# Moving attention heads by DMA into projection layout, and reordering the second layer's front, in a two-layer transformer kernel

## The reference

```
x  = hidden_states                        # 2048 x 256
xn = layernorm(x)
x  = x + attention0(xn) + moe0(xn)        # causal softmax attention, 16 heads of 16; 16 experts, top 2
xn = layernorm(x)
x  = x + attention1(xn) + moe1(xn)        # linear-type attention; 16 experts, top 4, and a shared expert

attention0: q, k, v = xn @ w_qkv.T; softmax(q k / 4, causal) v per head; heads side by side @ w_o.T
moe1:       probs = softmax(xn @ w_router); top 4, their weights divided by their sum
            out = shared / 5 + 4/5 * sum over the 4 chosen experts
```

## Time and profile before

| | us |
|---|---|
| median of 3 runs | 920.88 (918.10 to 924.36) |
| profiled execution, its own time | 918.57 |
| span of the profiled execution | 916.8 |
| stage 1 ends (last copy of ps_o) at | 593.75 |
| stage 2 runs from | 596.51 |
| stage 2 ends, first matmul of stage 3 at | 739.57 |
| granted TensorE clock, mean | 0.962 |

### The profile page before, as it was taken

The page is one execution under the profiler, slowest core; times in us unless marked ns, Lnnn a source line. Parts: engine busy times, 40 slices in busy tenths (PEclk is TensorE's granted clock), DMA queues, the critical chain, the costliest instruction groups (busy, mean ns, idle before and its releaser), DMA issues. The chain is left out here.

```text
span 916.8 us, 16029 instructions
## 1 busy us (share of the span) xinstructions
PE 844.7 (92%) x4769; PEld 455.6 (50%) x4770; DVE 641.0 (70%) x1513; ACT 451.3 (49%) x820; POOL 434.7 (47%) x720
## 2 busy tenths in 40 slices
PE   5888789899999999999999997698899989999997
PEld 3533223334444444444444321187744468878886
DVE  5589799888788888888788893167737524445448
ACT  3643145466666566665666666634113123333347
POOL 3323064613644435445345455401777737778820
PEclk9997598999999999999999999987999989999999
DMA  9744952200271211621111012192252234555566
GB/s 328 213 136 138 217 123 76 86 27 30 90 125 35 65 37 53 118 68 42 59 37 48 30 58 75 41 342 78 95 186 92 81 97 154 155 161 155 156 249 245
DMA packets 61730, 105.41 MB, mean 115 GB/s; under 512 B 12118, under 2 KB 45398, under 8 KB 60886
## 3 DMA queue, kind: packets, MB, share of 16 engines
q1 hardware_dynamic: 41110, 49.57, 19.8%
q0 software_dynamic: 16000, 45.70, 14.8%
q10 hardware_dynamic: 4544, 9.21, 3.3%
HBM read 60.30 MB, written 45.96 MB: 116 GB/s over the span
## 5 line engine op out<-in xcount | busy, mean ns | idle before, releaser
L1143 DVE TENSOR_REDUCE part_max<-ps_row 128x1 f32<-128x512 f32 (+3 forms) x560 | 354.1, 671 | 69.8 <-PE ps_row L1297 40.5
L1013 ACT ACTIVATE probs<-ps_st 128x1024 f32<-128x1024 f32 (+3 forms) x320 | 278.4, 896 | 202.3 <-PE ps_st L1276 201.0
L1201 PE MATMUL ps_o<-probs,v_all 128*17 128x512 f32 (+3 forms) x1280 | 148.5, 536 | 13.9 <-ACT probs L1013 8.5
L1297 PE MATMUL ps_row<-ks,qs 96*128 96x512 bf16 (+3 forms) x320 | 110.5, 380 | 11.7 <-DVE part_max L1143 8.6
L1297 PE MATMUL ps_row<-xt_ks,qs 96*128 96x512 bf16 (+3 forms) x320 | 103.2, 351 | 1.0 <-DVE part_max L1143 0.5
L1540 POOL DMA_INDIRECT yd<-moe_ys,moe_home x79 | 82.3, 1042 | 29.8 <-POOL moe_home L1534 17.2
L1276 PE MATMUL ps_st<-qs,ks 99*128 99x512 bf16 (+3 forms) x320 | 88.9, 360 | 4.4 <-DMA qs<-max_parts 4.2
L1276 PE MATMUL ps_st<-qs,xt_ks 99*128 99x512 bf16 (+3 forms) x320 | 82.8, 348 | 2.1 <-ACT probs L1013 1.3
L1571 PE MATMUL moe_ps_h<-w,moe_xs_t 128*128 x316 | 83.0, 386 | 0.1
L1297 PEld LDWEIGHTS ps_row<-ks,qs 96*128 96x128 bf16 x320 | 32.0, 101 | 93.6 <-DVE part_max L1143 57.2
L885 POOL TENSOR_SCALAR_AFFINE_SELECT probs<-probs 128x256 f32<-128x256 f32 x128 | 52.1, 414 | 49.4 <-ACT probs L1013 48.0
(11 more groups left out here) (290 smaller groups left out, 1349.0 us busy)
## 6 DMA issues: line engine op xcount, KB each, us to landing
moe_xs<-xd SPq DMA_DIRECT2D x79, 129.0 KB
qk_parts<-probs SPq DMA_DIRECT2D x16, 384.0 KB, 3.3
qs<-qk_parts SPq DMA_DIRECT2D x96, 64.0 KB, 2.4
moe_xs<-xd POOLq DMA_DIRECT2D x47, 128.0 KB, 2.4
yd<-moe_ys POOLq DMA_DIRECT2D x47, 128.0 KB, 2.1
xd<-zeros POOLq DMA_DIRECT2D x2, 2048.0 KB, 15.4
moe_w<-in_w ACTq DMA_DIRECT2D x2, 2048.0 KB, 20.1
w<-in_we SPq DMA_DIRECT2D x1, 4096.0 KB, 19.3
```

The source lines that it names most:

```text
L1013: act.activation(probs[:, at % NPB, :, off:CH], ps_st[at % 2][:, :, off:CH], ACT.Exp, scale=HD ** -0.5).then_inc(exp_done, 1)
L1143: dve.tensor_reduce(part_max[reduced % 2][:, h:h + k, i, j:j + 1], bank[:, 0:k * w].rearrange("p (h w) -> p h w", h=k), AX_X, ALU.max).the ...
L1201: mm = pe.matmul(ps_o[32 * q:32 * q + HD + 1, off:CH], m.v_all[:, k, g * HG + q, :], probs[:, (at + q // 2) % NPB, q % 2, off:CH], start=F ...
L1297: mm = pe.matmul(cols, qs[c][0:KROWS, h, i * P:(i + 1) * P], ks[g % 2][0:KROWS, h, j * CH:j * CH + w], start=True, stop=(j < c))
```

## The change

- Stage 1: ACT copies `ps_o` to one small tile `o_now` instead of into `o_t`. SP then moves the four heads by four DMAs to the partitions that the projection wants, and the four rows of divisors by four DMAs to DRAM (`heads_home`); the next copy waits for them. When the two groups of a projection half are there for a chunk (8 "shares" in all), SP gathers the 4096 divisors as 128x32 (`gather`), DVE inverts them in place (`invert`), SP writes them back (`return`) and spreads them over the heads' partitions in eight DMAs (`spread`), and DVE multiplies (`share`). These five steps stand 3, 6, 7, 10 and 13 exps after the pair's end in the list. The last share is done in stage 2. `w_o` is loaded in stage 1, by two DMAs ahead of the first gather.
- Planner: SP is charged 3.6 for the moves, and once all max rows and moe0 tiles are placed, the rank of an exp is 1 in place of 3 or 0.
- Stage 2: the two transposes, the reciprocals, the division and ACT's copy go; PE projects straight from `o_t` in two alternating banks. Router picks come from the logits, the exponential of the 16 x 4 chosen ones is taken once at the end, the counts are summed over the four choices by matmul. Order of PE, DVE and ACT is written anew. SP's large weight loads come after the last share's DMAs. Two shared units move behind the tail.
- The barriers at the ends of stages 1 and 2 no longer drain GpSimd.

```diff
+SHARE_STEPS = (("gather", 3), ("invert", 6), ("return", 7), ("spread", 10), ("share", 13))
+def heads_home(eng, m, g, c):
+    k, half, cs = g // 2, g % 2, slice(c * CH, (c + 1) * CH)
+    for h in range(HG):
+        home = (half * HG + h) * HD
+        eng.dma_start(m.o_t[home:home + HD, 2 * k, cs], m.o_now[32 * h:32 * h + HD, :]).then_inc(m.o_moved, 16)
+    for h in range(HG):
+        eng.dma_start(m.den[k * C + c, (half * HG + h) * CH:(half * HG + h + 1) * CH].unsqueeze(0),
+                      m.o_now[32 * h + HD:32 * h + HD + 1, :]).then_inc(m.o_moved, 16)
+def gather_divisors(eng, m, n):
+    eng.wait_ge(m.o_moved, MOVES * ((2 * k + 1) * C + c + 1))
+    eng.dma_start(m.divisor, m.den[n, :].rearrange("(p j) -> p j", p=P)).then_inc(m.o_hops, 16)
+def return_divisors(eng, m, n):
+    eng.wait_ge(m.inverted, n + 1)
+    eng.dma_start(m.rec[n, :].rearrange("(p j) -> p j", p=P), m.divisor).then_inc(m.o_hops, 16)
+def spread_divisors(eng, m, n):
+    eng.wait_ge(m.o_hops, HOPS * n + 32)
+    for h in range(NH // 2):
+        eng.dma_start(m.o_t[h * HD:(h + 1) * HD, 2 * k + 1, c * CH:(c + 1) * CH],
+                      m.rec[n, h * CH:(h + 1) * CH].unsqueeze(0).to_broadcast([HD, CH])).then_inc(m.o_hops, 16)
+def invert_divisors(dve, m, n):
+    dve.wait_ge(m.o_hops, HOPS * n + 16)
+    dve.reciprocal(m.divisor, m.divisor).then_inc(m.inverted, 1)
+def share_heads(dve, m, n):
+    dve.wait_ge(m.o_hops, HOPS * (n + 1))
+    dve.tensor_tensor(m.o_t[:, 2 * k, cs], m.o_t[:, 2 * k, cs], m.o_t[:, 2 * k + 1, cs], ALU.mult).then_inc(m.shared, 1)
...
-        rank = {"exp": 3 if busy[0] else 0, "pv": 2 if at["exp"] - 2 * at["pv"] < PV_LAG + 1 else 0.2,
+        alone = at["row"] == len(rows) and at["moe"] == len(moe)
+        rank = {"exp": 1 if alone else 3 if busy[0] else 0, "pv": 2 if at["exp"] - 2 * at["pv"] < PV_LAG + 1 else 0.2,
...
-        block = ctx.enter_context(nc.Block())
+        block = ctx.enter_context(nc.Block(no_gpsimd_drain=True))
...
                         load_queries(sp, m, g + 1, c, q_in[c])
+                    sp.wait_ge(o_copied, g * C + c + 1)
+                    heads_home(sp, m, g, c)
+                elif u[0] == "gather":
+                    if u[1] == 0:
+                        sp.wait_ge(slots_ready, TOP0 + 1)
+                        for k in range(KH):
+                            sp.dma_start(m.wo[k], a["w_o_t"][k * P:(k + 1) * P, :]).then_inc(m.wo_in, 16)
+                    gather_divisors(sp, m, u[1])
...
-                act.copy(m.o_t[:, g, c * CH:(c + 1) * CH], ps_o[:, :]).then_inc(o_copied, 1)
+                if (g, c) != (0, 0):
+                    act.wait_ge(m.o_moved, MOVES * (g * C + c))
+                act.copy(m.o_now, ps_o[:, :]).then_inc(o_copied, 1)
...
+            def project(tiles):
+                for i in tiles:
+                    pe.wait_ge(m.shared, C + i // TC + 1)
+                    if i >= 2:
+                        pe.wait_ge(added, i - 1)
                     for k in range(KH):
-                        mm = pe.matmul(ps_w, heads_t[:, j % 2, k, :], wo[:, k, :],
+                        mm = pe.matmul(ps_w[i % 2], m.o_t[:, 2 * k, i * P:(i + 1) * P], m.wo[k],
                                        start=(k == 0), stop=(k == KH - 1))
...
+            for i in range(0, 5):
+                tile(i)
+            invert_divisors(dve, m, last)
+            scales(0)
+            for i in range(5, 9):
+                tile(i)
+            scales(1)
+            tile(9)
+            share_heads(dve, m, last)
+            best_of(0)
+            tile(10)
+            slots_of(0)
...
+            pe.wait_ge(m.wo_in, 16 * KH)
+            project(range(0, 6))
+            turn(range(0, 2))
+            project(range(6, 7))
+            turn(range(2, 4))
+            project(range(7, 10))
```

More of the change, by code:

```diff
@@ L560, in place_pv @@
                 end["q", g + 1, c] = run("SP", 3.0, ("pv", m)) + LANDED
+            run("SP", MOVED, ("out", at["out"] - 1))
     def place_row(after):
@@ L652, in attention_plan, with with_shares @@
     return plan
+SHARE_STEPS = (("gather", 3), ("invert", 6), ("return", 7), ("spread", 10), ("share", 13))
+def with_shares(plan):
+    exps = [u for u in plan if u[0] == "exp"]
+    due, at, n = [], 0, 0
+    for u in plan:
+        if u[0] == "exp":
+            at += 1
+        elif u[0] == "pv":
+            g, c, k, _ = exps[2 * u[1]][1:]
+            if g % 2 and k == TC * (c + 1) - 1 and n + 1 < len(SHARES):
+                assert SHARES[n] == (g // 2, c)
+                due += [(at + later, name, n) for name, later in SHARE_STEPS]
+                n += 1
+    due.sort(key=lambda step: step[0])
+    out, at = [], 0
+    for u in plan:
+        out.append(u)
+        if u[0] == "exp":
+            at += 1
+            while due and due[0][0] <= at:
+                out.append(due.pop(0)[1:])
+    return out + [step[1:] for step in due]
@@ new lines, in _ @@
+            project(range(0, 6))
[3 more added lines that the diff above has]
+            project(range(7, 10))
+            pe.wait_ge(w_in, 32)
+            pe.wait_ge(ones_ready, 1)
+            score(range(0, 4))
+            project(range(10, 11))
+            add_gram(range(0, 2))
+            turn(range(4, 6))
+            add_gram(range(2, 3))
+            turn(range(6, 8))
+            ranks(0)
+            project(range(11, 12))
+            score(range(4, 8))
@@ L2072, in _ @@
+            add_gram(range(3, 5))
+            project(range(12, 14))
+            add_gram(range(5, 6))
+            project(range(14, 15))
+            turn(range(8, 10))
+            add_gram(range(6, 7))
+            project(range(15, 16))
+            turn(range(10, 12))
+            ranks(1)
+            score(range(8, 12))
+            add_gram(range(7, 10))
             turn(range(12, 14))
-            add_gram(range(6, 7))
+            add_gram(range(10, 11))
             turn(range(14, 16))
-            add_gram(range(7, 8))
@@ L2124, in _ @@
             mm.then_inc(norms_done, 1)
-            for n in range(4, len(units)):
+            for n in range(4, TAIL_BEFORE):
                 shared(n)
@@ L2134, in _ @@
                 mm.then_inc(tail_done, 1)
+            for n in range(TAIL_BEFORE, len(units)):
+                shared(n)
 def two_layers(nc, a, out):
```

325 lines of the change are left out of this document (135 added, 190 removed).

## The result

The changed kernel takes 943.07 us, median of 4 runs (939.75 to 947.26), against 922.42 for the kernel before (918.10 to 924.36); the ratio is 1.023 with a 95% interval of 1.018 to 1.029. It is slower by 2.3%. Forecast were 945 us and slower. The profiled execution has a span of 941.1 us, against 916.8. The experiments ran on three chips; on the second and third the kernel before itself takes some 970 us because of its stage 2, in some executions more than in others, so what ran there is compared by stretches of stage 1.

The account below looks back on a forecast made before the run. PE was taken to bound stage 1, DVE a close second, and the chain to POOL's dispatch stage 2. Terms summed to +24.0 us on the profiled 918.57, giving 942.6, or 945 for the median; range 910 to 957.

Parts of the forecast that it names:

- The tail: Last pair of stage 1: new rank cuts the period of two exponentials from 2.70 to 2.05 us, -6.5 us.
- The two long waits: Stage 1, shares 0 and 3: gather and spreads land late behind key loads, so PE waits; +14.8 and +16.5 us.
- The mechanism behind them: SP's queue in stage 1: small transfers issued behind large key loads wait for those to land; gather near 272.
- The clock: After the two long PE idle times, some 6 us at half clock each, costing 3 us each: +6 us.
- Short waits: Stage 1, other shares: inversions and products each short by 0.7 to 0.9 us, mostly covered: +2 us, bounds 0 and 8.
- More work: Stage 1: seven reciprocals and seven products, 6.3 us of DVE, mainly hidden in its free time: +2 us.
- Stage ends: Ends of stages 1 and 2: last homes +3.7, GpSimd drains gone -1.6, together +2.1 us.
- The front: Start of stage 2 to POOL's first dispatch cast: 25.5 us in place of 41.4, -15.9 us.
- Bulk loads: Stage 2: SP's later weight loads fall on the first dispatches, +3 us, bounds 0 and 6.
- its own lower end: Low end of the forecast's own range for the whole kernel: 928 us, with waits at two thirds and clock 2.
- Rival A: Stage 1: gather and spreads overtake the keys, long waits fall from 31.3 to 9.3 us; 918 us, chance 0.15.
- Rival B: Stage 1: slack hides DVE's waits, idle under 2 us at each of fourteen steps; 904 us, chance 0.17.

Follow-up runs that it names:

- keys_on_act: Changed kernel with the key loads of groups 2 and 3 issued from ScalarE's queue instead of SP's: 932.28 us, ratio to before 1.012.
- the first experiment: Changed kernel with the keys of groups 2 and 3 issued behind the spreads of shares 0 and 3: 922.92 us, ratio to before 1.002.
- no_hops: As the first experiment, but gather, reciprocal, return, spread and product of shares 0 to 6 left out: 903.77 us, ratio to before 0.980.
- drains_kept: Changed kernel with both stage ends draining GpSimd again: 978.67 us where before took 969.79, ratio 1.008.
- keys_and_steps: As the first experiment, with steps at 5, 10, 11, 13, 22 exps and gathers waiting for earlier spreads: 908.40, 908.59, 945.23, 946.59 us.
- before_rank: The kernel before with only the changed kernel's new rank of an exp: 964.06 us against 969.79, ratio 0.993.

## Why the prediction was right

Slower was forecast at 945, and 943.07 was measured. By its terms:

*The tail.* -6.5 forecast. The period is 2.08 us, 2.05 forecast, but the last pair became only 4.2 shorter (33.1 us after 37.3), since its first microseconds have idle times of ACT of some 2 us that the steady period doesn't know.

*The two long waits.* 14.8 + 16.5 forecast for PE, 13.78 and 13.23 measured. At share 0 the reciprocal was forecast at 272 and ran at 271.3. At share 3 the size was off by 3 us: the product ran at 417.5, but DVE came to it later than forecast, at 403.5, because of the waits before. The keys had landed after 11.0 us at most, not 13.5. The price of each in all is larger than PE's idle: from pair (1,0)'s copy to (1,1)'s the time grows by 16.7 us, and from (2,0)'s to (2,1)'s by 17.8, so 2.9 and 4.6 us beside the idle times. Nearly all of that is the clock, as told below.

*The mechanism behind them* was only half right. I argued from w_router that a small transfer waits behind a large one of its own queue. keys_on_act shows that it waits as well when the large one is on another queue. The changed kernel can't tell the two apart, and the forecast didn't need to. Where it mattered was the first experiment, whose size I missed by 12 to 18 us.

*The clock.* 6 forecast, 7.1 measured: the 2.5 and 4.6 us by which the same matmuls keep PE busy longer in the two pairs. The granted clock is 0.50 from PE's first matmul after the wait until about 277.3 and 424, 5.1 and 5.5 us, which cost about half of that each, 2.5 and 2.7; so the forecast of 3 each was close behind the long waits. The other 1.9 us of the second pair stand ahead of its long wait, in a stretch that the forecast did not have. DVE's late reciprocal before share 3 left PE idle for only 1.88 us at 390, and the clock reads 0.50 from about 393 to 397:

```profile
391.85 0.69 PE L1459 MATMUL ps_row<-moe_w,moe_hid_t 128*128 x2 [1.88 <-DVE part_max L1266]
```

```profile
394.00:396.00 2.00, 2.00 (x10) 1.51 (x9) 1.48 (x5) 1.53 (x2) 0.68 (x2) 0.50 0.80 194
```

So a short wait, too, can cost as much again in clock as it does in idle time.

*Short waits.* 2 forecast. DVE waited 20.8 - 15.1 = 5.7 us at five more reciprocals, the longest 2.06 before share 3's, around which the distance from (1,3) to (2,0) grows by 2.1 us; another 2.1 are lost between (1,1) and (1,3), where the next reciprocals wait: 4.2 in all, twice the forecast and within its bounds. One more microsecond between (3,1) and (3,2) stands in no_hops too, so it is not the waits'. Where no wait fell, nothing was lost: from the copy of (2,1) to that of (3,1) both kernels take 125.5 us (521.61 - 396.14 before, 560.49 - 434.97 after), with share 4's five steps and 32 moves within them.

*More work.* 2 forecast, 0 by the same stretch, 1 with the microsecond from (3,1) to (3,2).

*Stage ends.* 2.1 forecast, +1.7 and -3.3 measured. The homes' 3.7 us cost 1.7, and the 0.8 that I gave to the drain of stage 1 is nothing by drains_kept. The 3.3 at the end of stage 2 I had not priced, and their cause is not shown. PE is done long before POOL now (idle for 13.0 us ahead of stage 3, 4.3 before), so the end follows the dispatch alone. But before, too, DVE's last work ended (736.04) only 0.7 us after SP's loads had been issued, and POOL's first instruction of stage 3 came 3.3 us later (739.31), where now it comes 0.5 us after SP's last issue (762.17, 762.67). The missing drain may be in that; no run separates it.

*The front.* 15.9 forecast, 16.7 measured. Ranks of the first chunk stand at 655.95, 21.9 us after PE's start, with a wait of 2.18 us for the first xn where 2.4 was forecast.

*Bulk loads.* 3 forecast, 6.2 measured, just above the bound of 6.

The misses cancel. Against the forecast the result is better by 4.3 at the long waits, 3.8 at the stage ends and 0.8 at the front, and worse by 2.3 at the tail, 3 at clock, short waits and added work, 3.2 at the loads and 0.8 in stage 3: together +0.4, as 24.3 is to 24.0. That the sum came within 2 us is luck; the terms were off by up to 4. One sum of the prediction is wrong: its own lower end, waits at two thirds and a clock of 2, is 945 - 10.4 - 4 = 930.6 and not 928. Nothing turns on it.

Rival A (small transfers overtake) falls by the 11.7 us of a gather of 16 KB. Rival B gave 904 for waits that cost nothing. The waits did cost: its condition, under 2 us at each of the fourteen steps, wasn't met. Its time is near what the kernel takes once the waits are gone: 908.4 in keys_and_steps, which does all the work, and 903.8 in no_hops, which leaves a part of it out.

## What to carry to other kernels

A chain of small transfers, with an engine's wait for it at a fixed place in that engine's order, can cost much by its place and little by its work. Before putting the wait, look up what else is under way on the DMA engines then, on any queue, and put the step behind its landing. Here the inversion moved from 6 to 16 exps after its pair's end and the product from 13 to 24, which gave back 32 us, and the steps' own work cost under 2.5. Count the clock with the wait: after PE idle times of 2 to 4 us it cost about 2 us more. When a wait is removed by moving the large transfer, look at the next small one behind it.

## What the runs showed of the hardware

While the six key loads of 256 KB are under way, the 16 DMA engines show a share of 1.06 and 1.00 for 10 us at only 125 and 117 GB/s. In stage 2 of the kernel before, while SP's weights are loaded, a share of 1.07 goes with 413 GB/s:

```profile
605.00:610.00 5.00, 5.00 (x33) 4.25 (x32) 4.19 (x17) 2.49 (x5) 0.00 (x0) 1.00 1.07 413
```

A full share is thus not a full rate.

In before_rank the stretch from the first cast to SP's moe1 loads took 136.2 us (634.85 to 771.03) where before took 95.4, while stage 1 ran as in before. DVE and ACT have long idle times there for which the profile finds no event of this core ("remote"), and PE waits for both engines. The traces of before and after have no such time. In before_rank, by line (us, times, longest):

```profile
DVE o_t L1902 <- remote: 35.4, 1, 35.4
DVE given L262 <- remote: 25.9, 3, 12.1
```

```profile
ACT gram L1783 <- remote: 39.6, 1, 39.6
```

The cause is open.
